# Query and key projections done by head pairs inside the attention, wide fillers in the routing, and the norm's scale and bias taken into the gate weights

## The reference, cut to what matters

```python
x = x + gcn2(relu(gcn1(layernorm(x))))                    # 625 x 768
# transformer block on layernorm(x)[None]; 12 heads of 64
h = _ln(x, ln1_g, ln1_b)
q = einsum('btd,hds->bhts', h, Wq); k = ... Wk; v = ... Wv
att = softmax(where(causal, q @ k.T * 768 ** -0.5, -inf))
x = x + (att @ v).reshape(b, t, d) @ Wp + bp
h2 = _ln(x, ln2_g, ln2_b)
w, sel = top_k(h2 @ Wg, 1); w = softmax(w)
y = relu(h2 @ W1[e] + b1[e]) @ W2[e] + b2[e]              # for the chosen expert e
x = x + w * y
```

## Time and profile before

| | |
|---|---|
| median of 3 runs | 905.63 us |
| the profiled execution | 904.44 us |
| its span | 902.6 us |
| mean granted TensorE clock | 0.985 of 2.4 GHz |
| PE busy / weight loads (PEld) busy | 856.0 us (95%) / 824.7 us (91%) |
| VectorE (DVE) / ScalarE (ACT) busy | 708.9 us (79%) / 556.7 us (62%) |
| GpSimd (POOL) busy | 78.1 us (9%) |
| moved by DMA | 196 MB, 217 GB/s in the mean |
| chain that ended last | PE 53%, DVE 25%, DMA 10%, issue 6%, ACT 5% |

### The profile page before, as it was taken

One profiled execution on the slowest core, in us unless ns is written; L12 is line 12 of the kernel. 1 busy time (PEld: TensorE's weight loads), 2 busy tenths in 40 slices (PEclk: granted clock), 3 DMA queues, 4 the chain that ended last, 5 costly groups with the idle time before them and its releaser, 6 DMA issues.

```text
span 902.6 us, 14661 instructions
## 1 busy us (share of the span) xinstructions
PE 856.0 (95%) x5386; PEld 824.7 (91%) x5386; DVE 708.9 (79%) x1069; ACT 556.7 (62%) x781; POOL 78.1 (9%) x83
## 2 busy tenths in 40 slices
PE   7999999899997888899899999999999999999997
PEld 7999999899995776799899999999999999999996
DVE  7999585872227889944779798898989989898995
ACT  4513241362227888823678787887888888788770
POOL 2000000230004100012240000000000000000040
PEclk9999999999999999999799999999999999999997
DMA  7030027174318600330399999999999999999974
GB/s 233 3 106 1 19 44 144 41 185 77 105 54 235 235 2 1 85 107 1 99 353 337 377 337 368 353 360 378 346 382 371 359 371 354 376 353 373 369 264 127
DMA packets 116007, 195.99 MB, mean 217 GB/s; under 512 B 33828, under 2 KB 83196, under 8 KB 115958
## 3 DMA queue, kind: packets, MB, share of 16 engines
q1 hardware_dynamic: 107796, 169.08, 55.8%
q0 software_dynamic: 6336, 24.19, 7.9%
q10 hardware_dynamic: 1826, 2.06, 0.8%
HBM read 177.40 MB, written 17.90 MB: 216 GB/s over the span
## 4 chain that ended last, share of the span: by engine, by line
PE 53%; DVE 25%; DMA 10%; issue 6%; ACT 5%; SPq 0%; DVEq 0%; ACTq 0%
PE ps L1361 13%; DVE wlo L905 11%; PE ps L1735 10%; DMA raw<-in_L_ffn_W 9%; PE ps L1716 8%; PE ps L1537 7%; PE ps L1442 2%; PE ps L1468 2%; DVE pr L1129 2%; ACT whi L602 2%; PE ps L1597 2%; DVE pTl L905 2%; PE ps L1390 2%; DVE hTT L903 1%; PE ps L1574 1%
## 5 line engine op out<-in xcount | busy, mean ns | idle before, releaser
L905 DVE TENSOR_TENSOR wlo<-raw,whi 128x2304 fp32r<-128x2304 f32 x137 | 348.3, 2551 | 21.3 <-ACT whi L602 21.0
L602 ACT ACTIVATE whi<-raw 128x2304 fp32r<-128x2304 f32 x139 | 296.1, 2132 | 79.3 <-DMA raw<-in_L_ffn_W 31.2
L1735 PE MATMUL ps<-whi,hTT 128*128 128x384 f32 x768 | 201.6, 339 | 1.0 <-ACT oh7T L602 1.0
L1735 PEld LDWEIGHTS ps<-whi,hTT 128*128 128x128 f32 x768 | 139.1, 188 | 1.2 <-ACT oh7T L602 1.2
L1716 PE MATMUL ps<-whi,hgh 128*128 128x384 f32 x384 | 132.8, 346 | 1.3 <-DVE hgl L905 1.3
L1735 PE MATMUL ps<-wlo,hTT 128*128 128x384 f32 x384 | 129.0, 336 | 0.0
L1716 PE MATMUL ps<-whi,hgl 128*128 128x384 f32 x384 | 128.9, 336 | 0.0
L1716 PE MATMUL ps<-wlo,hgh 128*128 128x384 f32 x384 | 128.5, 335 | 0.0
L1716 PEld LDWEIGHTS ps<-whi,hgh 128*128 128x128 f32 x384 | 72.2, 188 | 1.5 <-DVE hgl L905 1.5
L1716 PEld LDWEIGHTS ps<-wlo,hgh 128*128 128x128 f32 x384 | 72.3, 188 | 0.0
L1735 PEld LDWEIGHTS ps<-wlo,hTT 128*128 128x128 f32 x384 | 72.3, 188 | 0.0
(11 more groups left out here) (285 smaller groups left out, 1715.5 us busy)
## 6 DMA issues: line engine op xcount, KB each, us to landing
raw<-in_L_ffn_W SPq DMA_DIRECT2D x128, 1152.0 KB, 6.9
hs_d<-bc POOLq DMA_DIRECT2D x13, 384.0 KB, 6.4
raw<-in_L_gnn_W SPq DMA_DIRECT2D x4, 1152.0 KB, 5.8
hs<-hs_d POOLq DMA_DIRECT2D x8, 384.0 KB, 5.5
ys_d<-ysb POOLq DMA_DIRECT2D x7, 384.0 KB, 6.1
raw<-in_L_ffn_Wv SPq DMA_DIRECT2D x6, 384.0 KB, 5.3
raw<-in_L_ffn_Wq SPq DMA_DIRECT2D x6, 384.0 KB, 5.3
raw<-in_L_ffn_Wk SPq DMA_DIRECT2D x6, 384.0 KB, 5.2
```

Source lines behind the costliest of these rows:

```text
L602: act.activation(out_, in_, func).then_inc(s, 1)
L905: dve.tensor_tensor(out_, in_, hi_, ALU.subtract).then_inc(s, 1)
L1735: ins = mm(ps[0:CAP, 4 + half, 0:HB], l, rr, start=k == 0 and j == 0 and jj == 0, stop=k == FCH - 1 and j == JW - 1 and jj == 2)
```

## The change

1. Queries and keys are projected in the same groups of 18 products, but by head pairs (`qk_products(g)`, g = 4m + 2r + half, r = 0 for queries and 1 for keys). Groups 0 to 3 stand before the attention. Groups 4 to 23 stand in the attention, one in step -1 and one in each step i up to 23 whose c is not 0, behind the turns and ahead of the values (`next_pair(i)`). Pair m + 1 is made during pair m. All of them use bank 6, one after the other.
2. Their weights come and are split by head pair and matrix in "units" of 768 columns (12 units, 6 places in the two `raw` buffers) instead of eight half matrices of 2304 columns: 6 units before the attention, 6 in steps 1, 4, 6, 9, 11 and 14. The copies out (`qk_out(g)`) have 314 columns. Keys are kept for two pairs only (`k_[m % 2]`).
3. Wp is split in four parts of 1152 columns in steps 24 to 27 (`wp_hi`, `wp_lo`). Before, its two halves were split in the key projection and ahead of the first maximum.
4. `turn_last` uses bank 4 or 5 and waits for the low part of the same step's first head (`s_trl`); in the first step of a pair the second maximum on VectorE stands behind the second `turned`. The fillers of steps 0 and 1 are gone.
5. `h2T` is copied by two ScalarE instructions (4 and 2 blocks) without scale and bias. The scale is multiplied into the gate weights once (`wgs`), the bias goes through the gate in six small products ahead of the projection (`gbias`) and is added where the logits are read.
6. The fillers of the routing are 512 columns wide, in `float32r`, 14, 4, 8 and 12 of them in place of 24, 24 and 30 narrow ones; the 4 stand between the gate products of the last two chunks.
7. The zeros for the dispatch buffers in memory are written after group 3, `xfb` is loaded in two parts in the attention, `base` after it. Buffers move between regions to make room.

The core of the diff:

```diff
-FRONT = 12
-PAIR_FRONT = {(0, 1): 8, (0, 3): 9, (1, 1): 10}
+FRONT = 8
+UNIT_AT = {1: 6, 4: 7, 6: 8, 9: 9, 11: 10, 14: 11}
+QK = 3 * DC
+QK_LATE = {4: 0, 1: 1, 2: 2, 3: 3}
+WP_AT = STEPS - 6
-TURN_BUSY = 24
-CHOICE_BUSY = 30
+NORM_BUSY, GATE_BUSY, RANK_BUSY, CHOICE_BUSY = 14, 4, 8, 12
...
+        def qk_part(g):
+            return ps[:, 6 if g >= 4 else g, 0:HALF]
+        def window_pair(i):
+            return (i + 1) // C + 1
...
@@ scalar
+            def unit_hi(j):
+                a.wait_ge(s_unit[j % UNIT_PLACES], 32 * (j // UNIT_PLACES + 1))
...
+                hi(unit(j, front_w)[0], raw_unit(j), s_uhi)
+            def qk_out(g):
+                a.wait_ge(s_pj, C + g + 1)
...
+                hi(qk_home(g, 0), qk_part(g), s_pjh)
...
             for i in range(STEPS + 3):
                 if i < STEPS:
                     exponent(2 * i)
                     exponent(2 * i + 1)
+                if i == 0:
+                    qk_out(4)
                 if 1 <= i <= STEPS:
                     turned(2 * i - 2)
                     turned(2 * i - 1)
...
+                if i in UNIT_AT:
+                    unit_hi(UNIT_AT[i])
+                if 0 <= i - WP_AT < WP_PARTS:
+                    wp_hi(i - WP_AT)
+                if i % C in QK_LATE and window_pair(i) < PAIRS:
+                    qk_out(4 * window_pair(i) + QK_LATE[i % C])
                 if 2 <= i < STEPS + 2:
                     heads_out(i - 2)
...
             def h2_turned(c):
                 a.wait_ge(s_n2T, c + 1)
-                for m in range(DC):
-                    act.activation(h2T[:, m, c * P:(c + 1) * P], blocks(0, 128, DC, P)[:, m, :], ACT.Identity,
-                                   scale=lnT[:, 2 * DC + m:2 * DC + m + 1],
-                                   bias=lnT[:, 3 * DC + m:3 * DC + m + 1]).then_inc(s_h2T, 1)
+                for m0, m1 in ((0, 4), (4, DC)):
+                    act.activation(h2T[:, m0:m1, c * P:(c + 1) * P], blocks(0, 128, DC, P)[:, m0:m1, :], ACT.Copy
+                                   ).then_inc(s_h2T, 1)
...
@@ tensor
-            for r, w in enumerate((WQ, WK)):
-                pe.wait_ge(*split(2 * w + 2))
-                for m in range(PAIRS):
...
+            def qk_products(g):
+                m, r, half = g // 4, g // 2 % 2, g % 2
+                pe.wait_ge(s_ulo, unit_count(g // 2))
+                if g >= 4:
+                    pe.wait_ge(s_pjl, C + g)
...
+                for a_ in range(QK):
+                    c, i = divmod(a_, 3)
...
+                    ins = mm(qk_part(g), l, rr, start=a_ == 0, stop=a_ == QK - 1)
+                ins.then_inc(s_pj, 1)
+            def next_pair(i):
+                if i % C in QK_LATE and window_pair(i) < PAIRS:
+                    qk_products(4 * window_pair(i) + QK_LATE[i % C])
...
             def turn_last(t):
-                if t >= C:
-                    pe.wait_ge(s_trl5, t // C)
+                pe.wait_ge(s_trl, 2 * t + 1)
...
             scores(0)
+            next_pair(-1)
             for i in range(STEPS + 2):
                 if i + 1 < STEPS:
                     scores(i + 1)
-                    if i < 2:
-                        keep_busy(FILL_BUSY, k_[0][:, 0, 0:128], k_[0][:, 0, 0:512])
...
                 if 1 <= i <= STEPS:
                     turn(2 * i - 2)
                     turn(2 * i - 1)
-                    if i % C == 0:
-                        turn_last(i - 1)
+                if 1 <= i <= STEPS and i % C == 0:
+                    turn_last(i - 1)
+                next_pair(i)
                 if i >= 2:
                     values(i - 2)
...
-            keep_busy(TURN_BUSY, onesb[:, :], onesb[:, :], 3)
+            held = front_w[1][0]
+            keep_busy(NORM_BUSY, held[:, 0:128], held[:, 0:512], 3)
             turn_n2(C - 1)
             gate_products(C - 2)
+            keep_busy(GATE_BUSY, held[:, 0:128], held[:, 0:512], 3)
             gate_products(C - 1).then_inc(s_gate, 1)
-            keep_busy(TURN_BUSY, onesb[:, :], onesb[:, :], 3)
+            keep_busy(RANK_BUSY, held[:, 0:128], held[:, 0:512], 3)
```

More of the change, by code:

```diff
@@ L68 @@
 EARLY_X = 3
-FILL_BUSY = 8
 STEPS = PAIRS * C
+WP_AT = STEPS - 6
 PRS = 5
@@ L198, in build @@
         raw += [R1["raw2"], R1["raw3"]]
-        front_w = [(whi[i], wlo[i]) for i in range(F_SLOTS)] + [(R2["whif"], R2["wlof"])]
+        front_w = [(whi[i], wlo[i]) for i in range(F_SLOTS)]
         whi += [R0["whi3"]]
@@ L310, in build @@
         s_fhi, s_flo = sem("front_hi"), sem("front_lo")
+        s_unit = [sem(f"qk_weight_in{p}") for p in range(UNIT_PLACES)]
+        s_uhi, s_ulo = sem("qk_weight_hi"), sem("qk_weight_lo")
         s_var, s_root = sem("variances_made"), sem("roots_made")
@@ L1152, in _ @@
             for i in range(STEPS + 3):
+                late = i % C == 0 and i
                 if i + 1 < STEPS:
                     maximum(2 * i + 2)
-                    maximum(2 * i + 3)
+                    if not late:
+                        maximum(2 * i + 3)
+                if i == 0:
+                    qk_out(4)
                 if 1 <= i <= STEPS:
```

261 lines of the change are left out of this document (170 added, 91 removed).

## The result

The changed kernel took 898.25 us, the median of 8 runs (895.83 to 902.21), beside 908.12 us (904.86 to 911.13) for 8 runs of the kernel before: a ratio of 0.9909, 95% interval [0.9892, 0.9926]. A second comparison later gave 900.40 against 906.06 us, 0.9938 [0.9915, 0.9962]. 893.5 us had been predicted, 0.9866 of the median shown then (905.63 us). The sign was right; the predicted gain of 12.1 us is 2.3 to 6.5 us larger than the measured ones of 9.9 and 5.7 us.

The account below looks back on a forecast made before the run. PE replaces VectorE as the attention's bound. The stretch: 15.9 + 116.3 + 1.1 + 21.4 + 11.9 = 166.6 against 177.3 us, 10.7 less; with routing's 1.2, 904.44 becomes 892.5, median about 893.5, range 882 to 903 us.

Parts of the forecast that it names:

- The projection before the attention is gone, four groups of 10.4 us stay.: Query and key projection: four groups of 2.61 us stay ahead, 10.4 us; 20 move into the attention.
- The bias products: Gate's bias products at the start of the new stretch: 1.4 us, bounded by the gate products' 1.37.
- PE takes over as the bound, pairs of 25.3 us.: First five head pairs: PE load 22.4 plus changes of kind 0.9 and waits 0.4 and 1.6, 25.3 us.
- `turn_last` waits 1.6 us in each pair.: Each pair: low part of chunk 4's first head comes after 3.0 us, PE has work for 1.4; wait 1.6.
- The last pair.: Steps 24 to 27, no group: 13.3 us before, Wp parts add 5.1 and DVE waiting 3.0; together 21.4.
- From step 28's maximum to Wp as now: 11.9.: Attention's tail, last maximum to first Wp product: taken over unchanged from the old profile, 11.9 us.
- The routing, 1.2 us less.: Gate products of chunk 4 at full clock end at 432.8, not 434.0: 1.2 us less, range 0 to 2.5.
- The experts: Expert stage: runs at its DMA limit from its start, shifted as a whole, length unchanged.
- the forecast's own 888 to 898: Whole kernel: the main forecast case, 888 to 898 us, chance 0.50.
- the third rival: Attention pairs: groups cost more than PE's waiting, a wait in each step, periods 27.7 us; 898 to 906 us, chance 0.22.
- The second rival: Attention pairs: PE's load alone sets them, 22.4 to 23.3 us; whole kernel 878 to 888 us, chance 0.20.
- The fourth: New attention: the lower clock holds; half of steps 1 to 23 so loses 29 us, time 922; chance 0.08.

Follow-up runs that it names:

- e1_bank6: The changed kernel with the fifth blocks turned in bank 6 again, so `turn_last` no longer waits for its step's first head's low part: 891.19 us, ratio 0.9827.
- e8_bank6_wp26: The changed kernel with the fifth blocks in bank 6 and the four Wp parts in steps 26 to 29 instead of 24 to 27: 889.61 us, ratio 0.9794.
- e3_tail_fill: The changed kernel with six 512-column fillers in each of steps 24 to 29, ahead of transposes and values: 899.37 us, ratio 0.9913.
- e7_bank6_fill: The changed kernel with the fifth blocks in bank 6 and six fillers in each of steps 27 to 29: 888.36 us, ratio 0.9784.
- e11_before_h2T: The kernel before with only the two-instruction `h2T` copy, without scale and bias; tokens choose other experts and one overflows: 1159.24 us, ratio 1.2797.
- e4_narrow: The changed kernel with the old 125-column routing fillers, 24, 0, 24 and 30 of them: 894.81 us, ratio 0.9865.
- e9: The changed kernel with bank 6 for `turn_last`, fillers in steps 27 to 29, Wp parts two steps later and narrow routing fillers: 888.98 us, ratio 0.9809.
- e0_after: The changed kernel run again, unchanged, in a later set: 900.40 us, ratio 0.9938 to the kernel before.

## Why the prediction was right, and where it was off

Its own steps, in order:

- **The projection before the attention is gone, four groups of 10.4 us stay.** Measured 10.55. The bias products took 1.21, predicted 1.4. From the end of the values' projection to the first maximum of 625 keys the sum had 26.8 us (15.9, two steps of 5.4 and 4.4, and VectorE's lag of 1.1), the trace 27.9: 1.1 short.
- **PE takes over as the bound, pairs of 25.3 us.** Measured 25.6 (the two maxima in the rows below are 25.67 apart), with weight loads of 22.0 (predicted 22.4), DVE 19.7 (19.1) and ACT 18.0 (18.1). The full clock was assumed and is there, 1.00 in each. Four periods are 1.3 us over.

```profile
238.79 0.81 DVE L1234 CUSTOM_DVE_ANT_0 pr<-ps,cmask 125x626 f32<-125x626 f32 x1
264.46 0.81 DVE L1234 CUSTOM_DVE_ANT_0 pr<-ps,cmask 125x626 f32<-125x626 f32 x1
```

- **`turn_last` waits 1.6 us in each pair.** 1.28 in the row above, 1.33 in the mean of all six; taking it away gave 1.3 a period.
- **The last pair.** 26.7 in the sum (5.3 and 21.4), 26.95 measured. The size was right by luck, for three terms were off and cancel. The four Wp parts had 8.1 us (5.1 and 3.0 for their order); by e1_bank6 and e8_bank6_wp26 two parts cost 3.05, so four some 6.1, an estimate. Without parts the sum had 18.6 us, where the old pair and one group make 17.3 + 2.6 = 19.9. And the fifth `turn_last` stands in these steps and was not in the sum: 1.0 (26.95 against 25.91 in e1_bank6).
- **"From step 28's maximum to Wp as now: 11.9."** This is the step that failed: 15.2 us. The tail was taken over unchanged, though it holds the sixth `turn_last` with the very wait that the prediction had priced for the others: 1.2 us (e3_tail_fill against e7_bank6_fill, both at the full clock). The other 2 us or so are the clock, 0.75 over the window shown above. That part is no effect of the change alone: 11.9 was read from the one profile of the kernel before that kept the full clock there, and the two other profiles of the same attention have tails of 12.8 and 13.1. The four profiles of the changed tail have 13.7 to 15.0, 14.5 in the mean against 12.6, so that 1.9 us are left for the change.
- **The routing, 1.2 us less.** 1.7 from Wp to the first expert product, 1.3 from norm to choice. The number is near and the mechanism is not. The prediction gave the gain to the gate products' clock, thanks to the wide fillers, and let the short copy count for nothing ahead of the transposes. The short copy alone brings 2.15 (e11_before_h2T), 3.0 with the clock held; the wide fillers then cost 1.7 (e4_narrow). It had seen the 14 fillers as late by 0.2 us; they are late by 0.7.
- **The experts** keep their length, within the 3.7 us by which it varies from one execution to the next.

The misses, 1.1 + 1.3 + 0.25 + 3.3, make 5.9 us: the whole way from the 166.6 predicted to the 172.5 of the trace. The measured 898.25 and 900.40 lie just above the forecast's own 888 to 898, and inside the range of 882 to 903. They fall into the interval of the third rival (898 to 906), but only by number: its periods of 27.7 us with a wait in each step did not come. Two slips of the prediction have no weight in it: the first maximum came 5.2 us after the projection's end, not 5.5, and the chances of being faster by more than 0.5% add up to 0.81, not 0.82.

The second rival (PE's load alone sets the pair, 22.4 to 23.3 us) did not come either: even with the wait gone, e1_bank6 has 24.3 us against loads of 22.1. The Trainium skill ("Perfetto Trace Analysis", Identifying the Most-Contended Engine) judges TensorE's headroom by the busy time of its weight loads, beside the share of peak work. In this trace that finds the right engine, and it is not the period: 3.6 us lay above the loads, 2.2 of them still with bank 6. The fourth (the lower clock in the attention) did not come in the first five pairs; it is 1.00 from 238.8 to 353.2. In each of the eight profiles of the changed kernel and its variants without fillers in the attention the clock fell in the attention for the first time in the last pair, behind the last group of 18 products, and in the three with fillers in the last steps (e3, e7, e9) it did not fall in the attention at all. That agrees with the rule of the Trainium skill ("TensorE: Matmul & The Clock Gate", Part 1) that activity releases the throttle.

## What to carry to other kernels

A wait that is found by hand is also a question to the program: `turn_last` stood in the forecast with 1.6 us a pair (1.3 measured), and moving two small blocks to another bank took 7 to 9 us off the median (898.25 and 900.40 against 891.19), about as much again as the whole change had brought. When a stretch is rebuilt, price its tail again instead of carrying it over, since the same new waits reach into it, and read it from more than one profile, since the clock alone moves such a tail by more than 1 us. A filler has to fit into an idle that the trace shows. In the routing the fillers cost what they outlast it by (0.7 us) and, between two steps of the path, all that they take (1.0 us); none at all costs as much up to the choice and more behind it, through the clock.

## What the runs showed of the hardware that was not expected

- Fillers get longer with the fall that they are to prevent: 12 of 512 columns take 3.00 us or 4.67, 8 of them 2.11 us (in e0_after) or 3.56, 24 of 125 columns 1.56 or 2.80.
- Six ScalarE copies of 125 columns with scale and bias take 2.19 us, two copies of 500 and 250 columns together 0.86:

```profile
425.22 0.86 ACT L885 ACTIVATE h2T<-ps 128x500 f32<-128x500 f32 x2 [2.32 <-PE ps L1763]
```

- The same instructions meet the lower clock at another moment in each execution: the tail of the changed kernel was 15.0 us in one profile and 13.7 in the other, that of the kernel before 11.8, 12.8 and 13.1.
